# Unit 0's x in one transfer, two z copies ahead of an exponential, and a new written order of calls for the first units

## What is computed

```python
# step 1: x = x + attn(cond(x))
att   = softmax(gelu(gelu(cond_128 @ W0 + b0) @ W1 + b1) @ W2 + b2)        # 64 x 8
mixed = einsum('boi,bih->boh', einsum('bk,koi->boi', att, weight), x) + (att @ bias_k)[:, :, None]
q = einsum('bsD,Ddh->bsdh', mixed, Wq) + bq;  k, v likewise with one head
p = softmax(einsum('bsdh,bse->bsde', q, k) / sqrt(32))                     # summed over the 32 heads h
o = einsum('bsde,bse->bsd', p, v)                                          # 32 values, each repeated 32 times
x = x + broadcast(o)
# step 2: x = x + ffn(cond2(x))
c   = conv1d(x, 9 taps, 4 groups) + (cond_128 @ c_weight.T)[:, :, None] + fside[None, :, None]
x   = x + c @ (scale * (nibbles - zero_point)).T + bias
```

## Time and profile before

| | |
|---|---|
| time, median of 3 runs | 424.02 us (423.35 to 424.45) |
| profiled execution: its own time | 423.17 us |
| its span, first to last instruction | 421.4 us |
| TensorE busy (PE, matmul) | 407.5 us, 97% |
| GpSimd (POOL) | 357.1 us, 85% |
| VectorE (DVE) | 352.6 us, 84% |
| ScalarE (ACT) | 222.5 us, 53% |
| DMA | 79.13 MB, mean 188 GB/s |

### The profile page before, as it was taken

One profiled execution on the slowest core, in us unless ns is written; L12 is line 12 of the kernel. 1 busy time (PEld: TensorE's weight loads), 2 busy tenths in 40 slices (PEclk: granted clock), 3 DMA queues, 4 the chain that ended last, 5 costly groups with the idle time before them and its releaser, 6 DMA issues.

```text
span 421.4 us, 6619 instructions
## 1 busy us (share of the span) xinstructions
PE 407.5 (97%) x2133; PEld 345.5 (82%) x2133; DVE 352.6 (84%) x582; ACT 222.5 (53%) x471; POOL 357.1 (85%) x358
## 2 busy tenths in 40 slices
PE   4997999999999999999999999999999999999997
PEld 3996987888888887888888888888888888888886
DVE  2679799899999997896999999989889899983422
ACT  4624776546556463844474565546363556572700
POOL 6025999989999979999999999799989889999920
PEclk9999699999999999999999999999999999999999
DMA  8997967284721492633837472918092562726112
GB/s 278 414 381 264 329 233 278 55 324 155 276 81 49 152 309 94 207 102 93 337 80 251 133 297 72 342 40 300 10 316 112 119 212 64 268 50 228 51 52 101
DMA packets 22874, 79.13 MB, mean 188 GB/s; under 512 B 6056, under 2 KB 6696, under 8 KB 18856
## 3 DMA queue, kind: packets, MB, share of 16 engines
q1 hardware_dynamic: 22680, 78.32, 53.8%
q10 hardware_dynamic: 144, 0.13, 0.1%
HBM read 61.14 MB, written 17.30 MB: 186 GB/s over the span
## 4 chain that ended last, share of the span: by engine, by line
PE 60%; POOL 2%; DMA 2%; issue 0%; DVE 0%; POOLq 0%
PE p_f L1366 40%; PE p_conv L1360 15%; PE p_sm L1330 4%; DMA o_c<-o_dram 2%; PE p_sm L1345 1%; POOL c_lo L513 1%; POOL xc L503 1%; PE p_conv L1366 0%; POOL xn L531 0%; DMA o_dram<-o_sb 0%; POOL xc L506 0%; POOL xc L504 0%; DVE xn L1025 0%; DVE o_sb L1003 0%; POOLq L529 0%
## 5 line engine op out<-in xcount | busy, mean ns | idle before, releaser
L1366 PE MATMUL p_f<-w_ffn,u_hi 128*128 128x512 f32 (+1 forms) x512 | 195.0, 392 | 0.0
L1366 PE MATMUL p_f<-w_ffn,u_lo 128*128 128x512 f32 (+1 forms) x512 | 194.3, 389 | 0.0
L734 ACT ACTIVATE u_sb<-p_conv,u_bias,cols_sb 128x128 f32<-128x128 f32 x256 | 94.9, 459 | 41.0 <-PE p_conv L1360 40.9
L1366 PEld LDWEIGHTS p_f<-w_ffn,u_hi 128*128 128x128 f32 x512 | 96.3, 188 | 20.3
L1366 PEld LDWEIGHTS p_f<-w_ffn,u_lo 128*128 128x128 f32 x512 | 96.2, 188 | 19.9
L513 POOL TENSOR_TENSOR c_lo<-xc,c_hi 128x516 fp32r<-128x516 f32 (+1 forms) x68 | 84.2, 1248 | 4.3 <-POOL xc L506 0.9
L524 POOL TENSOR_TENSOR xn<-xn,bias_n 128x1024 f32<-128x1024 f32 x32 | 76.5, 2406 | 0.2
L724 ACT ACTIVATE c_hi<-xc 128x516 fp32r<-128x516 f32 (+1 forms) x68 | 41.2, 612 | 61.3 <-POOL xc L506 61.2
L503 POOL TENSOR_TENSOR xc<-xc,o_c 128x384 f32<-128x384 f32 (+1 forms) x68 | 58.0, 853 | 12.1 <-DMA o_c<-o_dram 10.4
L1011 DVE STREAM_TRANSPOSE p_ut<-u_sb 128x512 f32<-128x512 f32 (+1 forms) x68 | 46.0, 683 | 19.7 <-ACT u_sb L734 19.4
L531 POOL TENSOR_TENSOR xn<-xn,o_sb 128x1024 f32<-128x1024 f32 x32 | 61.0, 1921 | 0.3
(11 more groups left out here) (105 smaller groups left out, 474.8 us busy)
## 6 DMA issues: line engine op xcount, KB each, us to landing
xc<-xc_in_in SPq DMA_DIRECT2D x16, 1032.0 KB, 8.8
xn<-xn_in_in SPq DMA_DIRECT2D x16, 1024.0 KB, 7.2
out<-xn SPq DMA_DIRECT2D x31, 512.0 KB, 6.3
xt<-xt_in_in SPq DMA_DIRECT2D x15, 1024.0 KB, 7.2
o_c<-o_dram SPq DMA_DIRECT2D x15, 256.0 KB
xn<-wq_in SPq DMA_DIRECT2D x5, 512.0 KB, 10.6
xt<-wq_in SPq DMA_DIRECT2D x2, 512.0 KB, 4.9
xt<-xt_in_in SPq DMA_DIRECT2D x2, 512.0 KB, 8.1
```

What stands on the lines that cost most here:

```text
L734: ins = eng.activation(u_sb[:, g % 2, i * P:(i + 1) * P], p_conv[g % 2][:, i * P:(i + 1) * P], ACT.Identity, bias=u_bias[:, g, bat:bat + 1 ...
L1366: return mm(ffn_ps(k, part), u[:, (k // TU) % 2, r, t * P:(t + 1) * P], w_ffn[:, r, at:end], **flags)
```

## The change

The arithmetic is unchanged. What changes is one transfer, one deleted wait, and the order of the calls in the five lists.

Transfers and waits:

```diff
-            def load_first(h):
-                r = slice(h * R // 2, (h + 1) * R // 2)
-                eng.dma_start(xt[:, 0, r, :], xt_in[0, :, r, :]).then_inc(s_xt_first if h else s_x[0], 16)
-
...
             load_wvk()
-            load_first(0)
+            load_x(0)
             load_wq(2)
-            load_first(1)
             load_wq(3)
...
             load_x(1)
+            load_x(2)
             load_conv_weights()
-            load_x(2)
             load_x(3)
+            load_x(4)
             load_c(0)
-            load_x(4)
             save_o(0, 0)
             load_packed()
             spread_first(0)
             load_x(5)
+            load_n(0)
+            save_o(0, 1)
             load_x(6)
-            save_o(0, 1)
-            load_n(0)
             spread_first(1)
...
             def x_bias(k):
                 u = k // TU
-                if k % TU == 0 and u:
-                    eng.wait_ge(s_add, added(u + 1, G - 1))
...
-                if r == R // 2:
-                    eng.wait_ge(s_xt_first, 16)
```

GpSimd, the first calls:

```diff
             add_o(0, 0)
             add_o(0, 1)
+            c_low(0, 0)
+            c_low(0, 1)
             add_o(0, 2)
-            c_low(0, 0)
             subtract(1, 1)
             add_o(0, 3)
-            c_low(0, 1)
             c_low(0, 2)
-            c_low(0, 3)
             add_o(1, 0)
             add_o(1, 1)
+            c_low(0, 3)
+            c_low(1, 0)
```

ScalarE, the first calls:

```diff
             exp_att()
+            bias_of_u()
+            copy_vk()
             slices()
-            copy_vk()
-            bias_of_u()
+            keep_bias()
             mix_rows(0)
             mix_rows(1)
-            keep_bias()
+            mix_rows(2)
             keep_mix_bias()
-            mix_rows(2)
             mix_rows(3)
             z_copy(0)
+            z_copy(1)
             exp(0, 0)
-            z_copy(1)
             exp(0, 1)
+            z_copy(2)
+            z_copy(3)
             exp(1, 0)
             convert_weights(0, 0)
-            z_copy(2)
-            z_copy(3)
             c_high(0, 0)
+            c_high(0, 1)
             z_copy(4)
             convert_weights(0, 1)
-            c_high(0, 1)
+            u_copy(0, 0)
             c_high(0, 2)
-            exp(1, 1)
-            u_copy(0, 0)
-            c_high(0, 3)
             convert_weights(1, 0)
             u_copy(0, 1)
+            exp(1, 1)
             z_copy(5)
+            c_high(0, 3)
+            u_copy(0, 2)
```

VectorE, the first calls:

```diff
             logits()
+            mark_inexact()
             normal()
             sum_heads(1)
-            mark_inexact()
...
             low_nibbles()
             sum_v(0, 1)
+            sum_exp(1, 0)
             divide(0, 1)
             score(1, 1)
-            sum_exp(1, 0)
+            times_v(1, 0)
             high_nibbles()
-            times_v(1, 0)
```

TensorE, the first calls:

```diff
+            bias_rows()
             mlp(0)
             mlp(1)
-            bias_rows()
             mlp(2)
             context()
             turn_att()
-            read_flag()
+            keep_busy(6)
             mixing(0)
             mixing(1)
             mixing(2)
+            mixing_bias()
             mixing(3)
-            mixing_bias()
-            keep_busy(5)
             z_first(0)
+            read_flag()
             z_first(1)
...
             mix(2)
+            conv(0, 0)
+            conv(0, 1)
             project(5, 0)
-            conv(0, 0)
             project(5, 1)
-            conv(0, 1)
             conv(0, 2)
             project(6, 0)
+            project(6, 1)
             conv(0, 3)
-            project(6, 1)
+            conv(1, 0)
             project(7, 0)
-            conv(1, 0)
+            conv(1, 1)
+            mix(3)
+            conv(1, 2)
             linear(0, 0)
```

More of the change, by code:

```diff
@@ L432, in _ @@
             save_o(7, 1)
+            spread_o(7)
             store(9)
-            spread_o(7)
             load_n(7)
+            save_o(8, 0)
+            load_c(8)
+            save_o(8, 1)
+            load_x(12)
             store(10)
-            load_c(8)
-            load_x(12)
-            for i in range(8, NU + 2):
+            spread_o(8)
+            store(11)
+            load_c(9)
+            store(12)
+            load_n(8)
+            for i in range(9, NU + 2):
                 d = i - 2
@@ L598, in _ @@
             c_low(4, 2)
+            c_low(4, 3)
             x_bias(6)
-            c_low(4, 3)
             x_bias(7)
@@ L796, in _ @@
             exp(2, 0)
+            exp(2, 1)
+            c_high(1, 3)
+            u_copy(1, 2)
             c_high(2, 0)
             u_high(1, 0)
+            u_copy(1, 3)
             u_high(1, 1)
-            exp(2, 1)
+            u_high(1, 2)
             c_high(2, 1)
-            u_copy(1, 2)
-            u_copy(1, 3)
-            u_high(1, 2)
+            z_copy(7)
+            c_high(2, 2)
+            u_copy(2, 0)
             u_high(1, 3)
-            u_copy(2, 0)
+            c_high(2, 3)
@@ L807, in _ @@
+            u_high(2, 0)
             u_copy(2, 1)
-            c_high(2, 2)
-            u_high(2, 0)
-            c_high(2, 3)
+            u_copy(2, 2)
+            exp(3, 0)
             u_high(2, 1)
-            u_copy(2, 2)
+            u_high(2, 2)
             u_copy(2, 3)
-            u_high(2, 2)
-            z_copy(7)
+            exp(3, 1)
             u_high(2, 3)
-            exp(3, 0)
             c_high(3, 0)
-            exp(3, 1)
             c_high(3, 1)
             c_high(3, 2)
+            u_copy(3, 0)
@@ L882, in _ @@
             u_copy(7, 1)
-            c_high(7, 2)
             c_high(7, 3)
+            u_high(7, 1)
             u_copy(7, 2)
-            u_high(7, 1)
             u_high(7, 2)
             u_copy(7, 3)
+            u_high(7, 3)
+            c_high(8, 0)
             exp(8, 0)
-            u_high(7, 3)
-            for p in range(8, NP):
+            exp(8, 1)
+            c_high(8, 1)
+            c_high(8, 2)
+            z_copy(11)
+            c_high(8, 3)
+            u_copy(8, 0)
+            u_copy(8, 1)
+            u_high(8, 0)
+            u_high(8, 1)
+            u_copy(8, 2)
+            u_copy(8, 3)
+            u_high(8, 2)
+            u_high(8, 3)
+            exp(9, 0)
+            for p in range(9, NP):
                 a = unit_of(p) + 1
@@ L1531, in _ @@
             linear(0, 6)
+            project(7, 1)
+            conv(2, 0)
             linear(0, 7)
-            conv(2, 0)
+            project(8, 0)
             conv(2, 1)
             linear(1, 0)
+            mix(4)
+            conv(2, 2)
             linear(1, 1)
             linear(1, 2)
+            conv(2, 3)
             linear(1, 3)
@@ L1551, in _ @@
             linear(2, 4)
-            mix(4)
             linear(2, 5)
-            conv(3, 0)
             linear(2, 6)
@@ L1575, in _ @@
             linear(4, 4)
+            project(10, 0)
             linear(4, 5)
-            conv(4, 0)
             linear(4, 6)
-            project(9, 1)
+            conv(4, 1)
             linear(4, 7)
-            conv(4, 1)
             linear(5, 0)
+            mix(6)
             conv(4, 2)
@@ L1594, in _ @@
             linear(6, 0)
-            mix(6)
             linear(6, 1)
+            conv(5, 1)
             linear(6, 2)
-            conv(5, 1)
             linear(6, 3)
             linear(6, 4)
-            project(10, 1)
+            linear(6, 5)
+            linear(6, 6)
+            mix(7)
+            linear(6, 7)
             conv(5, 2)
-            linear(6, 5)
-            mix(7)
-            linear(6, 6)
-            linear(6, 7)
+            linear(7, 0)
             conv(5, 3)
-            linear(7, 0)
             linear(7, 1)
@@ L1620, in _ @@
             linear(8, 4)
+            conv(6, 0)
             linear(8, 5)
-            conv(6, 0)
+            linear(8, 6)
             conv(6, 1)
-            linear(8, 6)
             linear(8, 7)
```

381 lines of the change are left out of this document (199 added, 182 removed).

## The result

The changed kernel takes 427.43 us (median, 426.41 to 431.15) against 423.81 in the same comparison (422.14 to 424.80): 1.009 times the kernel before, 95% interval 1.0061 to 1.0119. It is slower by 3.6 us, where 1.2 us less was forecast. A second comparison of the same kernel gave 427.27 and 1.0113 (1.0067 to 1.0158). The ratios with their intervals are computed from the single runs of one comparison, without those in a slower state, and can differ by up to 0.3% from the quotient of the two medians.

A forecast was written before the change was run, and what follows sets the result against it. TensorE was taken as the bound, busy 407.5 of 421.4 us. Gains of 0.4 us up to linear(0, 0) and 0.8 us from small later stalls sum to 1.2: 424.02 - 1.2 = 422.8 us, range 420.3 to 425.5.

The forecast's parts named there:

- The moved loads and stores up to pass 8: Transfers reordered in the early passes: taken to cost or gain nothing, bounded by 1 us on either side.
- The prediction's own sign of being wrong: Forecast wrong if the clock doesn't fall, TensorE restarts over 1 us off, or has new waits over 1 us after 60.
- From there to the end it runs almost without a break: From project(5, 0) at 42.35 us in the kernel before, TensorE was said to work almost without idle time.
- the resume: TensorE starting work again after its early stall: forecast at 42.6 us with conv(0, 0), instead of 42.35, 0.25 us later.
- the sooner rise: Rival: the clock, fallen near 42 us, is up again at 46.2 instead of 49.5, worth 1.7 us: 421.1 us; chance 0.20.
- The start: Up to z of unit 0: z_first(7) at 20.4 instead of 21.79, z 1.4 us sooner, project(1, 0) only 0.6 sooner.
- The z copies: Copies for units 2 and 3 done by 34.4: mix(2)'s 2.69 us wait goes, TensorE idles 38.1 to 42.6 for c_low(0, 0).
- `linear(0, 0)`: Its start, after the first convolutions and projections: forecast at 60.4 us against a like point of 60.8, 0.4 us sooner.
- The start stays slow: Rival: the rounds of z of unit 0 run at the low clock, attention starts 2.0 us later: 426.0 us; chance 0.09.
- The u chain binds: Rival: u_low(0, 3), in time by 0.1 us, comes late, with a 1 us middle stall: 425.2 us or more; chance 0.09.
- Nothing comes of it: Rival: mix(2) moves into idle time, small stalls only change places: some 423.9 us; chance 0.18.
- The stalls after 60 us: TensorE's small waits for c_low and hidden ones like them, some 1.6 us: half taken to go, 0.8 us.

The follow-up runs named there:

- the opposite test: Kernel before, with unit 4's o put behind store(3) and load_n(4), and store(4) ahead of spread_o(4), on SyncE's list: 424.18 us, 1.0016.

## Why the prediction was wrong

**The step that failed** is "The moved loads and stores up to pass 8 I take at nothing, bounded by 1 us on either side". They cost 3.6 us. With o's two trips put ahead of the large transfers again the time was that of the kernel before, 1.0017; a single moved call, `load_n(4)`, is enough (1.0009). The prediction's own sign of being wrong, a new wait of TensorE over 1 us after 60 us, came twice, with 1.9 and 2.9 us. I had looked at the first loads of the list only and at when unit 6's x is wanted, not at which call on SyncE's list waits for what and who stands behind it. The rows to look at were there: SyncE's own waits, above all those of `load_n` for stores, and o's trip, which took 7.3 us from divide to `add_o`. That GpSimd had no idle time in front shows only that o came in time, not by how much. It was some 0.5 us, by an estimate: in the opposite test the way back took 4.9 us (`spread_o(4)` at 124.41, `add_o(5, 0)` released at 129.33), and from 123.65 that ends at 128.6, against 129.10.

**The second wrong step** is "From there to the end it runs almost without a break", taken to mean that work ahead of the resume decides alone. Filling the waits of the kernel before removed all 6.8 us of half clock and brought 1.0004, and filling them with o first 1.0011. TensorE without idle time in its rows wasn't alone in being late; the chain through `c_low` was as late, hidden behind a TensorE at half speed. So the prices put on the clock, 1.7 us for the sooner rise among them, had no ground: no run shows a gain from them. By these runs that rival wouldn't have given 421.1 either.

**The start** was right in direction and place: the dummies filled the wait, `mixing(0)` came at 12.51 (12.5 forecast), the rounds at 14.49 (14.5 or 15.0). The clock rose at about 13.3 in the changed kernel's first profile, not at 17, and the last round started at 19.41, not 20.4, since the folds, 7.52 us without a break from 11.78, ended at 19.3. Of this, `project(1, 0)` got 22.25 in the first profile, 21.78 in the second (22.8 forecast).

**The z copies** did as forecast: no wait for `mix(2)`, one wait for `c_low(0, 0)` in its place. Its size was off in the first profile, 5.5 us with a resume at 44.8 against 42.6; in the second `mix(2)` started at 36.59 and the convolutions ran from about 40.9. The clock fell again, for 6.8 and 3.4 us.

**`linear(0, 0)`** was forecast for 60.4; it started at 62.1 in the first profile and at 57.67 in the second, 2.7 us ahead of the forecast and 3.1 us ahead of the like point of the kernel before (60.8). At `add_o(5, 0)` the same execution was 4.9 us behind it (134.0 against 129.1): the whole loss, and a lead besides, went between the two. Of that, 3.55 us are GpSimd's wait for o.

**Rivals.** "The start stays slow" was named with 0.09 and 426.0. Rounds at the low clock were seen, in one execution of another kernel, but they aren't the cause: the old start made the changed kernel no faster. "The u chain binds" gave 425.2 by a new stall in the middle; there was one, but for o, not for u. "Nothing comes of it" is what the kernel with one call moved back does (423.75).

**The range** of 420.3 to 425.5 rested on the 1 us taken for SyncE's list. The stalls after 60 us weren't halved, 0.8 us, but the waits for `c_low` there rose from 0.7 to 5.2 us.

**Two readings** in it are wrong without moving the sum. What it calls a quarter-unit projection is half a unit: x16 in the row, where a whole unit is the x32 at 23.40 (the 1.8 us are rightly half of that). And its equation for the slow start gives t = 20.1, not 19.9.

## What to carry to other kernels

Read a reordering queue by queue, and on the queue that only issues transfers ask of each moved call what it waits for and what small, urgent transfer stands behind it: a 1 MB load whose buffer is still being stored from holds a 16 KB result that is ready, here for some 2 us. Look also at how much later the result may come before anyone waits for it, here some 0.5 us. Where two engines are late together, removing the visible half (here a stretch at half clock) brings nothing, so test it before pricing it; dummy matmuls in the wait are a cheap test. Follow one event deep in the kernel, as `add_o(5, 0)` here, over all variants: it shows whether time is lost ahead of it or behind it, here to within some 3 us.

## What the runs showed of the hardware

The stretches at 0.50 in these profiles lasted 3.4 us (nine of them) or 6.8 us (eight), after listed waits of 1.0 to 6.4 us. Two executions of one kernel differed in it (6.8 and 3.4 us after the wait for `c_low(0, 0)` in the changed kernel), and also in whether the clock fell: after a wait of 1.89 us (99.2 us, first profile) it stayed at 1.00, after one of 1.97 us at the same convolution (95.0 us, second profile) it fell at 96.6. With the same calls in front, the first rise came between 12.5 and 14.6 us in nine profiles with the new start and at 21.5 us in the tenth. The windows of a profile show 1.00 ahead of the first rise, as at 16 to 20 us of the slow start, although the matmuls run at half speed there; only the distance from start to start tells.

```profile
16.00:20.00 4.00, 4.00 (x20) 4.00 (x20) 2.74 (x4) 3.83 (x8) 0.00 (x0) 1.00 1.04 414
```
